# Four banks for maxima and projections, two for scores, and a reordered attention and feed-forward start

## The reference

```
x = x + attn_a(layernorm(x))   # causal, 32 query heads of 16, one key and value head, alibi bias
x = x + ffn(layernorm(x))      # router picks 1 of 32 hidden units in each of 56 blocks
x = x + attn_b(layernorm(x))   # 32 query and 8 key heads of 128, rope, window of 128
x = x + ffn(layernorm(x))

scores = q @ k.T * 16**-0.5 + slope * (pos_k - pos_q), causal;  attn_a = softmax(scores) @ v @ Wo
inter  = z @ c1.T @ c2.T;  idx = argmax of each block of 32;  ffn = relu(z @ w1[idx]) @ w2[idx]
```

## Time and profile before

| | us |
|---|---|
| median of 3 runs | 3085.81 |
| profiled execution | 3086.43 |
| its span, first to last instruction | 3084.6 |
| causal attention, 0 to | 591.7 |
| first feed-forward's router result of batch 0, batch 1 | 624.8, 771.3 |
| second feed-forward's, batch 0, batch 1 | 2640.4, 2785.1 |
| mean granted TensorE clock | 0.936 of full |

### The profile page before, as it was taken

One profiled execution on the slowest core, in us unless ns is written; L12 is line 12 of the kernel. 1 busy time (PEld: TensorE's weight loads), 2 busy tenths in 40 slices (PEclk: granted clock), 3 DMA queues, 4 the chain that ended last, 5 costly groups with the idle time before them and its releaser, 6 DMA issues. The chain is left out here.

```text
span 3084.6 us, 41728 instructions
## 1 busy us (share of the span) xinstructions
PE 2678.1 (87%) x14452; PEld 2053.9 (67%) x14452; DVE 2074.2 (67%) x4129; ACT 1121.8 (36%) x2436; POOL 976.9 (32%) x716
## 2 busy tenths in 40 slices
PE   3879898567989979999999987999999998589899
PEld 2444454255767757888888865788888886467677
DVE  2745645255777577778778757777877875657766
ACT  1345345222122244444444434444444443221221
POOL 1112011134222234444444423444444441342222
PEclk7799899778999999999999999999999999789999
DMA  5133332400000011110101100111010101100000
GB/s 189 31 107 84 81 106 59 140 1 0 1 0 0 23 35 35 35 34 27 32 9 34 34 29 8 35 35 34 27 32 8 34 21 44 63 1 15 14 14 14
DMA packets 112462, 117.64 MB, mean 38 GB/s; under 512 B 7028, under 2 KB 83956, under 8 KB 112308
## 3 DMA queue, kind: packets, MB, share of 16 engines
q1 hardware_dynamic: 112340, 116.04, 12.4%
HBM read 93.21 MB, written 22.81 MB: 38 GB/s over the span
## 5 line engine op out<-in xcount | busy, mean ns | idle before, releaser
L1762 POOL TENSOR_TENSOR rope_straight<-rope_straight,rope_crossed 128x512 f32<-128x512 f32 x160 | 206.8, 1292 | 478.4 <-DVE rope_crossed L1571 478.4
L520 POOL TENSOR_TENSOR f_hidden_low<-f_hidden,f_hidden_high 128x512 fp32r<-128x512 f32 x112 | 144.3, 1288 | 603.0 <-ACT f_hidden_high L468 603.0
L1667 ACT ACTIVATE probs<-probs,exp_bias 128x256 f32<-128x256 f32 (+1 forms) x512 | 240.7, 471 | 167.9 <-DVE exp_bias L1553 167.5
L896 DVE TENSOR_REDUCE a_max<-a_work 128x1 f32<-128x384 f32 (+3 forms) x352 | 209.6, 637 | 115.6 <-PE a_work L787 108.2
L261 PE MATMUL f_hidden_sum<-f_z_high,f_w_high 128*128 128x512 f32 x448 | 195.4, 436 | 75.7 <-POOL f_w_low L539 64.3
L1001 ACT ACTIVATE a_probs<-a_scores 128x512 f32<-128x512 f32 x320 | 173.0, 599 | 172.8 <-PE a_scores L801 95.9
L1412 PE MATMUL proj<-y_high,wq_high 128*128 128x512 f32 x512 | 213.3, 417 | 18.4 <-DVE y_low L1541 12.0
L782 PE MATMUL a_work<-a_keys,a_queries 64*128 64x256 f32 (+3 forms) x512 | 148.9, 443 | 71.9 <-DMA a_queries<-a_q_stacked 40.4
L1412 PE MATMUL w_sum<-o_high,wo_high 128*128 128x512 f32 x512 | 203.8, 398 | 7.6 <-DVE xt L1595 4.7
L372 DVE SCALAR_TENSOR_TENSOR f_hidden<-f_hidden_sum,f_mask_turned 128x512 f32<-128x512 f32 x112 | 77.0, 687 | 189.3 <-ACT f_mask_turned L463 172.2
L1412 PE MATMUL proj<-y_low,wq_high 128*128 128x512 f32 x512 | 204.0, 398 | 0.0
(11 more groups left out here) (239 smaller groups left out, 7683.8 us busy)
## 6 DMA issues: line engine op xcount, KB each, us to landing
a_queries<-a_q_stacked SPq DMA_DIRECT2D x16, 1024.0 KB, 6.3
wq_raw<-in_L_attn_b_wq SPq DMA_DIRECT2D x32, 512.0 KB
wo_raw<-in_L_attn_b_wo SPq DMA_DIRECT2D x16, 1024.0 KB, 6.8
a_q_stacked<-a_q_part_high SPq DMA_DIRECT2D x32, 256.0 KB
f_w_raw<-in_L_ffn_w SPq DMA_DIRECT2D x14, 512.0 KB, 10.1
f_w_raw<-in_L_ffn_w2t SPq DMA_DIRECT2D x14, 512.0 KB, 10.9
xt<-n_L_attn_a_hidden_states SPq DMA_DIRECT2D x4, 1024.0 KB, 29.3
a_q_stacked<-a_q_part_low SPq DMA_DIRECT2D x16, 256.0 KB
```

What stands on the lines that cost most here:

```text
L520: e.tensor_tensor(hl[:, j % 2], hm[:, :], f32(hh[:, j % 2]), ALU.subtract).then_inc(hl_ready, 1)
L896: e.tensor_reduce(mx[:, t % 2, to:to + nh], bank, AX.X, ALU.max).then_inc(work_free[k], 1)
L1667: e.activation(part, part, ACT.Exp, bias=bias[:, n % 2, t:t + 1], scale=SM_SCALE, accum_out=total[:, n % 2, t:t + 1]).then_inc(exp_done, 1)
L1762: e.tensor_tensor(ra[:, slot], ra[:, slot], rb[:, slot], ALU.add).then_inc(roped, 1)
```

## The change

In both feed-forward stages: `first_router` takes the place of `router_first(None)`; z of the first batch is normalised in four pieces; the squares stand ahead of the router constants on ACT; the constants' low parts are made by POOL instead of DVE; the w1 splits run two chunks ahead, the w2 splits one as before.

In the causal attention: `WORK` 4 and `SCORE` 2; new `SEARCH`, `OPENS` and `CLOSES`, and a `SEARCH_FIRST` for batch 0; tile 1's maxima of batch 0 move into the loop; the layer norm of batch 1 stands ahead of the loop, that of batch b+2 in slots 12 to 17; SP's list is reordered and x is loaded in pieces; the last batch's first three query tiles (`EARLY` = 384 columns) are divided and projected (`WoA`) apart from the last one, whose sums go from SBUF to SBUF, with half of its stores issued by ACT.

```diff
@@ ffn, TensorE
+            def first_router():
+                bank, full = aux_write(e, None, "T")
+                e.wait_ge(c_low, 1)
+                for d in range(DT):
+                    e.wait_ge(zh_ready, d + 1)
+                    e.matmul(bank[0:CROWS, :], c1h[:, d, :], zh[:, d, :], start=d == 0, stop=False)
+                    e.matmul(bank[0:CROWS, :], c1l[:, d, :], zh[:, d, :], start=False, stop=False)
+                    e.wait_ge(zl_ready, d + 1)
+                    mm = e.matmul(bank[0:CROWS, :], c1h[:, d, :], zl[:, d, :], start=False, stop=d == DT - 1)
+                mm.then_inc(full, 1)
@@ ffn, ScalarE (high_w1) and GpSimd (low_w1), in a chunk
                     if first and c + 1 < NCH:
-                        high_w1(c + 1)
+                        if c + 2 < NCH:
+                            high_w1(c + 2)
                         high_w2(c + 1)
@@ ffn, ScalarE before the loop
-            e.wait_ge(c_in, 32)
-            e.copy(c1h[:, :, :], c1_raw[:, :, :]).then_inc(c_high, 1)
             for d in range(DT):
                 e.wait_ge(first_centred, d + 1)
                 e.activation(first_squares[d], zf[:, d], ACT.Square).then_inc(first_squared, 1)
+            e.wait_ge(c_in, 32)
+            e.copy(c1h[:, :, :], c1_raw[:, :, :]).then_inc(c_high, 1)
             e.copy(c2s[:, :], c2_raw[:, :]).then_inc(c_high, 1)
             seed(None)
             high_w1(0)
             high_z(None)
             high_t(None)
+            high_w1(1)
             high_w2(0)
@@ ffn, GpSimd before the loop
+            e.wait_ge(c_high, 1)
+            e.tensor_tensor(c1l[:, :, :], c1_raw[:, :, :], f32(c1h[:, :, :]), ALU.subtract).then_inc(c_low, 1)
+            e.wait_ge(c_high, 2)
...
+            e.tensor_tensor(c2s[rest, :], c2_raw[rest, :], f32(c2s[rest, :]), ALU.subtract).then_inc(c_low, 1)
             low_w1(0)
+            low_w1(1)
             low_w2(0)
@@ causal_attention
-WORK, SCORE = 3, 3
+WORK, SCORE = 4, 2
+EARLY = S - P
-        SEARCH = {0: (2, 4), 1: (2, 4), 2: (2, 4), 3: (2, 4), 4: (3, 3), 5: (3, 3), 6: (3, 3), 7: (3, 3), 8: (3, 2),
-                  9: (3, 2), 14: (4, 2), 15: (4, 2), 16: (5, 3), 17: (5, 3), 18: (5, 2)}
-        OPENS = {4: ("mT", 2), 9: ("Vt", 0), 10: ("mT", 3), 16: ("mT", 4), 19: ("mT", 5)}
-        CLOSES = {0: ("mean", 0), 3: ("var", 0), 7: ("KV", 0), 8: ("Q", 0), 9: ("Q", 1), 10: ("Q", 2), 11: ("Q", 3),
-                  12: ("Wo", 0), 13: ("Wo", 1), 14: ("Wo", 2), 15: ("Wo", 3)}
+        SEARCH = {0: (2, 2), 1: (2, 2), 2: (2, 2), 3: (3, 3), 4: (3, 2), 5: (3, 2), 6: (3, 3), 7: (3, 2), 8: (3, 2),
+                  9: (3, 2), 10: (4, 2), 11: (4, 2), 12: (5, 2), 13: (5, 2), 14: (5, 2), 15: (5, 2), 16: (6, 2),
+                  17: (6, 3), 18: (6, 2), 19: (6, 3)}
+        SEARCH_FIRST = SEARCH | {0: (1, 4), 1: (1, 4)} | {s: (2, 4) for s in range(2, 6)} | {s: (3, 4) for s in range(6, 10)}
+        OPENS = {3: ("mT", 2), 4: ("Vt", 0), 10: ("mT", 3), 13: ("mT", 4), 17: ("mT", 5)}
+        CLOSES = {0: ("KV", 0), 2: ("Q", 0), 3: ("Q", 1), 5: ("Q", 2), 7: ("Q", 3), 9: ("Wo", 0), 11: ("Wo", 1),
+                  12: ("mean", 0), 13: ("Wo", 2), 14: ("Wo", 3), 15: ("var", 0)}
@@ plan
+            yield "small", "mean", 1, 0
+            yield "small", "var", 1, 0
-            for t in range(2):
-                for i in range(MAX_PAIRS[t]):
-                    yield "max", 0, t, i
-                yield "small", "mT", 0, t
+            for i in range(MAX_PAIRS[0]):
+                yield "max", 0, 0, i
+            yield "small", "mT", 0, 0
...
+                    if b == 0 and s in (1, 5):
+                        yield "small", "mT", 0, 1 if s == 1 else 2
...
             yield "pv", NB - 1, QUADS - 1
+            for d in range(DT):
+                yield "small", "WoA", NB - 1, d
@@ causal_attention, VectorE: last batch and tail
+                    if b == NB - 1 and p == 28:
+                        e.wait_ge(o_stored[0], 16 * OUT_DMAS * 2 * NB)
+                        e.wait_ge(o_stored[1], 16 * OUT_DMAS * (2 * NB - 1))
+                        e.reciprocal(sums[0:96, :], sums[0:96, :]).then_inc(inv_ready, 1)
+            e.wait_ge(o_stored[1], 16 * OUT_DMAS * 2 * NB)
+            e.reciprocal(sums[96:, :], sums[96:, :]).then_inc(inv_ready, 1)
@@ causal_attention, ScalarE: tail
+            store_out(e, NB - 1, 3, 1)
+            for m in range(DT):
+                high_out(NB - 1, m, slice(0, EARLY))
@@ causal_attention, SyncE: the loop and the end
-            send_max(0, 1)
+            e.dma_start(wo_raw[:, :, :], wo.rearrange("(t p) n -> p t n", p=P)).then_inc(wo_in, 16)
+            load_x(2)
...
+                if more:
+                    send_keys(b + 1)
+                if b == 0:
+                    send_max(0, 1)
...
+            e.wait_ge(inv_ready, NB)
+            for m in range(DT):
+                e.wait_ge(at_low, (NB - 2) * DT + m + 1)
+            load_last([0, 1, 2])
+            store_out(e, NB - 1, 3, 0)
+            e.wait_ge(inv_ready, NB + 1)
+            load_last([3])
```

More of the change, by code:

```diff
@@ L622, in causal_attention @@
         x_in = [sem(f"x_landed{b}") for b in range(NB)]
+        x_first, ones_landed, eye_landed = [sem(f"x_first_landed{d}") for d in range(DT)], sem("ones_landed"), sem("eye_landed")
         x_summed, sq_ready, sq_added, centred = sem("x_summed"), sem("sq_ready"), sem("sq_added"), sem("centred")
@@ L648, in of_batch, with searches @@
                 return (kind, b + i // ST, i % ST) if b + i // ST < NB else None
-            return (kind, b + 1, i) if b + 1 < NB else None
-        def searches(b, s, part):
-            if s not in SEARCH:
-                return
-            t, n = SEARCH[s]
-            if b + t // ST >= NB:
-                return
-            done = sum(k for r, (u, k) in SEARCH.items() if u == t and r < s)
-            for i in range(n * part // 4, n * (part + 1) // 4):
-                yield "max", b + t // ST, t % ST, done + i
-        def plan():
+            ahead = 2 if kind in ("mean", "var") else 1
+            return (kind, b + ahead, i) if b + ahead < NB else None
+        def plan():
+            done = {}
+            def searches(b, s, part):
+                t, n = (SEARCH if b else SEARCH_FIRST).get(s, (0, 0))
+                tile = b + t // ST, t % ST
+                if tile[0] < NB:
+                    for _ in range(n * part // 4, n * (part + 1) // 4):
+                        done[tile] = done.get(tile, 0) + 1
+                        yield "max", *tile, done[tile] - 1
             yield "small", "mean", 0, 0
@@ L713, in heads_in, with store_out @@
             return 4 if t == 0 else 2 if t == 1 else 1
+        def store_out(e, b, qt, half):
+            par, q = qt % 2, slice(qt * P, (qt + 1) * P)
+            e.wait_ge(o_copied, b * 2 * ST + qt * 2 + half + 1)
+            for j in range(4):
+                row, first = col_tile(half, j), (HEADS * half + 4 * j)
+                to = o_dram[b, first * AD:(first + 4) * AD, q].rearrange("(h d) q -> d h q", d=AD)
+                e.dma_start(to, ot[row:row + AD, par, half]).then_inc(o_stored[par], 16)
+            if b == NB - 1:
+                e.wait_ge(inv_stored, 16 * (NB - 1))
+                to = sums[AH * qt + HEADS * half:AH * qt + HEADS * (half + 1), :]
+            else:
+                to = sums_dram[b, HEADS * half:HEADS * (half + 1), q]
+            if half:
+                for c in range(2):
+                    e.dma_start(to[8 - 8 * c:16 - 8 * c], ot[64 * c + AD:64 * (c + 1):32, par, half])\
+                        .then_inc(o_stored[par], 16)
+            else:
+                e.dma_start(to, ot[AD::32, par, half]).then_inc(o_stored[par], 16)
         block = st.enter_context(nc.Block())
@@ L833, in _ @@
                     weigh(*step)
-            tail = [*(x[:, :] for x in work), sbank[0][:, :]]
+            tail = [x[:, 0:P] for x in work]
             for k, bank in enumerate(work):
@@ L924, in _ @@
                         low_weights(2, wkvl[:, :, 32:KV], w_raw[:, :, NQ:NQ + AD], wkvh[:, :, 32:KV])
+                    if step in (["var", 0, 0], ["var", 1, 0]):
+                        inverse_std(step[1], chain)
+                        for d in range(DT):
+                            normalise(step[1], d)
                     if step == ["var", 0, 0]:
-                        inverse_std(0, chain)
-                        for d in range(DT):
-                            normalise(0, d)
+                        for d in range(1, DT, 2):
+                            e.wait_ge(zh_ready, d + 1)
+                            e.tensor_tensor(zl[:, d], zf[:, d], f32(zh[:, d]), ALU.subtract).then_inc(zl_ready, 1)
                 elif kind == "max":
@@ L1241, in _ @@
                     load_queries(b + 1, 1)
-                store_out(b, 2)
+                send_max(b, 3)
+                if b == 0:
+                    load_x(3)
                 if more:
                     load_queries(b + 1, 2)
```

(3 more changed lines are left out.)

263 lines of the change are left out of this document (139 added, 124 removed).

## The result

The kernel after takes 2989.73 us (median of 4 runs, 2985.85 to 2992.66), the kernel before 3086.65 beside it: ratio 0.9686, 95% interval 0.9669 to 0.9703. The forecast was 2953, so the direction and the large terms held, and of 133 us of gain 97 came. The measured time lies 3 us inside the upper edge of the stated range (2925 to 2993).

| stage | before | after | gain | forecast |
|---|---|---|---|---|
| causal attention, from 0 | 591.7 | 567.0 | 24.7 | 42.5 |
| first feed-forward, start | 33.1 | 28.8 | 4.3 | 6 |
| its first batch | 146.5 | 109.4 | 37.1 | 41.2 |
| window attention | 1547.9 | 1554.1 | -6.2 | 0 |
| second feed-forward, start (from its first centring) | 25.3 | 21.9 | 3.4 | 4.3 |

What follows compares the result with a forecast made beforehand. No engine is full over the whole span, so each stage was read alone. Gains of 41.2 + 39.2 + 6 + 4.3 + 11 + 8 + 14 + 5 + 4.5 = 133.2 us took 3086.4 to 2953; range 2925 to 2993.

Steps and rivals of the forecast that it cites:

- rival 2: Causal attention: two score banks and late turning of maxima eat the even search, attention gains nothing; 2992 us; chance 10%.
- w1 ahead: Both feed-forward stages: PE no longer waits for w1 splits, first batches come down towards the second; gain 41.2 + 39.2 us.
- I charge 3 us per stage: Feed-forward first batches: 3 us deducted per stage for sums of squares queued on POOL behind splits and the colder start.
- rival 1: Feed-forward first batches: DVE, its operations falling behind POOL's splits, becomes the bound; 32 us lost, 2985 us; chance 10%.
- Start of the feed-forward: Both feed-forward starts: router matmuls follow z quarter by quarter; gain 6 us in the first stage, 4.3 in the second.
- Kernel start and batch 0: Causal attention: earlier queries and first maxima, less late turning of maxima, end batch 0 at 211 instead of 222; gain 11 us.
- Batches 1 to 3: Causal attention: fewer waits for maxima, less two score banks' cost; gains of 8, 14 and 5 us, bounds together -10 and 45.
- even search: Attention batches: two or three pairs of maxima in all slots, instead of four in slots 0 to 3 and none in 10 to 13.
- only 1 to 2 us: Attention batches: with Q's last projection two slots ahead of use, 1 to 2 of 5.7 us of PE's query wait go.
- Tail: End of causal attention: three quarters of the columns come early, 30.2 us behind the last weighing instead of 34.8; gain 4.5 us.
- 1.5 for the last matmuls: Attention tail: 1.5 us for PE's last matmuls, one term of the 30.2 us behind the last weighing.
- PE would wait for exps at every pair: Rival 3, attention: PE waits for the pair before's exps at each of 160 pairs; 3161 us at worst; chance 2%.

Runs made afterwards that it cites:

- Experiment 9: Kernel after with each POOL low part of w1 and w2 made by two instructions of 512 columns instead of one of 1024: 2978.06 us, ratio 0.9647.
- experiment 6: Kernel after with ACT's copies of the last batch's outputs two pairs of scores later, from pair 14 instead of 12: 2979.42 us, ratio 0.9626.
- experiment 3: Kernel after with three banks for maxima and projections and three for scores, as before: 2990.46 us, ratio 0.9685.
- (4): Kernel before with four banks for maxima and projections and two for scores, nothing else: 3056.24 us, ratio 0.9905.
- 8: Kernel before with four and two banks and all of the feed-forward's edits, none of the attention's other edits: 2985.15 us, ratio 0.964.
- (7): Kernel after with the maxima spread over the slots as before, the first ten slots of batch 0 kept: 2989.74 us, ratio 0.9662.
- Experiment 5: Kernel after with DVE's last reciprocal ahead of its four additions of early results, own semaphores for the last quarter's loads: 2977.68 us, ratio 0.9633.
- experiments 2: Kernel before with w1 split one chunk further ahead in both feed-forward stages and nothing else: 3011.10 us, ratio 0.9759.
- experiments 1: Kernel before with all of the feed-forward's edits and none of the attention's: 3013.77 us, ratio 0.9756.
- experiment 11: Kernel after with the start of the feed-forward as before, w1 staying one chunk ahead: 2986.09 us, ratio 0.9671.

## Why the prediction was right in kind, and its gain 36 us too high

The four figures to explain are 17.8 us of gain that the attention lacks, 9.5 that the two first batches lack, 2.6 that the starts lack, and 6.2 that the window attention lost. That rival 2's number, 2992, is nearer to the measured one than 2953 is chance: its terms (w1 in full, the attention at nothing) did not come.

**w1 ahead: mechanism right, the charge for the lock too small.** "I charge 3 us per stage" was read from the later chunks, where one operation falls behind one split. It was 7.1 (44.2 - 37.1) and 8.4: in the first two chunks POOL's list (two splits, then, in chunk 0, three sums) runs without a gap and catches two operations of one chain, and there PE has no lead. Experiment 9 shows it: halves give back 4.9 and 6.0. It is rival 1, at a third of its price: `L385` averaged 1.37 us in the first stage's first batch (0.85 with halves), over its mark of 1.3, `L358`'s successor 1.03.

**Start of the feed-forward:** 4.3 and 3.4 against 6 and 4.3, as said.

**Kernel start and batch 0:** 16.2 against 11. First scores at 82.4 (forecast near 80), and the batch took 123.4 us (forecast 131); the waits for landing maxima were 3.8, 3.9 and 1.5 us, less than the 6 each that were charged.

**Batches 1 to 3: the failed part.** 0.5, 13.4 and -2.5 against 8, 14 and 5. The forecast listed what moved in DVE's, PE's and SP's lists but not ACT's copies of the outputs, from pair 16 to 12, ahead of the loads they need: SP issues `load_out` behind stores and sends, and POOL's first product was ready 3.6 us late. That is 10.5 us of PE's waits (2.64, 3.89, 3.93); in experiment 6 the longest is 1.0, and batches 1 and 2 are 11.0 us shorter together. Second, it took bank split and even search for two gains. They are two cures of one wait: the max steps stand 27.1 us for `a_max` before, 12.6 with the new search and three banks (experiment 3), 6.9 with the banks alone (4) and 4.5 with both. In time, with the old search the banks bring 29 to 36 us (experiments 4 and 8), with the new one nothing (3), and the search with four banks nothing (7). Third, the wait for queries went from slot 14 to slot 10 with the maxima that need them, at 12.0 and 11.2 us for the slot, as the text had said that "only 1 to 2 us" would go.

**Tail:** -2.9 against 4.5. The step that failed is "1.5 for the last matmuls": the terms before it came out (9.3 us to the early matmuls, 10.3 for them, 5.0 instead of 7.3 from the reciprocal to the last ones), but these took 10.5, and 5.5 even at full clock. The order of DVE's program was seen rightly (the reciprocal did stand behind four additions, at 550.03), but not what it does to PE: 6.6 us idle, and then 48 matmuls at half clock (1.2 GHz). Experiment 5.

**Not forecast:** 6.2 us in the window attention, whose code is the same. Its cause is open (below).

**Readings that were off, without weight in the sum:** PE is busy 82.5% in batch 0, not 87 to 91 (99.5 of 120.6 us); and `L365` ended 0.55 us behind `L539`, not 0.4. Its argument that "one wait covers one split" did not hold in the chunk shown above, where two waits covered two splits.

The rival that the attention gains nothing fell as a whole (24.7 us came), though for batches 1 and 3 and the tail taken together it was right. That PE would wait for exps at every pair fell too: 24.6 us in 31 pieces over 160 pairs.

## What to carry to other kernels

Two edits that cure the same wait don't add: try each alone before both are costed, and let more buffers stand first, as it is the simpler. Of a reordered list, follow every engine's copy of it to the instruction that waits for a transfer: an instruction put too early on an in-order engine (a copy on ACT, four additions on DVE) stops all that stands behind it, and where PE stood long it pays again at the lower clock (the tail). Where POOL and DVE share a stretch, try POOL's long operations in two: here two stages gained 4.9 and 6.0 us by it.

## What the runs showed of the hardware

A matmul of 128 columns was 0.11 us behind the one before at full clock (experiment 5) and 0.21 at half, and those of 256 columns in the window attention of the kernel after were 0.12 apart: halving the columns from 256 saved next to nothing, so the 48 late matmuls of the tail are dearer than their columns tell.

The window attention took 1547.9, 1547.8 and 1548.0 us in before and experiments 2 and 4, and 1550 to 1561 in all others. Some of its pieces can be seen. One is four DVE operations, of which POOL's split catches the last or not. It is caught in experiments 1 and 8 alone, twice in each. Before, and in experiment 1:

```profile
1172.05 1.08 DVE L1560 TENSOR_SCALAR probs<-probs,exp_sum_inverse 128x128 f32<-128x128 f32 x4
1172.82 2.56 POOL L1769 TENSOR_TENSOR wkv_low<-wkv_raw,wkv_high 128x1024 fp32r<-128x1024 f32 x1 [3.05 <-ACT wkv_high L1690]
```

```profile
1130.88 3.27 DVE L1588 TENSOR_SCALAR probs<-probs,exp_sum_inverse 128x128 f32<-128x128 f32 x4
1131.65 2.35 POOL L1797 TENSOR_TENSOR wkv_low<-wkv_raw,wkv_high 128x1024 fp32r<-128x1024 f32 x1 [3.05 <-ACT wkv_high L1718]
```

The last of the four started 0.04 us ahead of POOL in the first and 0.06 behind it in the second, and took 0.35 or 2.44 us. In the kernel after it is not caught. There, a matmul group at the border of two batches started 6.8 us late with nothing in the trace to wait for, against 3.8 before. It was 6.6 to 7.2 us late in every kernel that has both the new attention and the new start of the feed-forward, and 3.8 to 4.2 in every kernel that lacks either. The other piece is the clock: the same 8008 matmuls kept PE busy 6.7 us longer, at a clock of 0.98 instead of 0.99. Before and after:

```profile
1067.10:2615.10 1548.00, 1433.88 (x8008) 1204.06 (x8008) 1178.39 (x2882) 674.41 (x1690) 620.73 (x464) 0.99 0.09 28
1001.10:2555.20 1554.10, 1440.60 (x8008) 1209.46 (x8008) 1177.91 (x2881) 674.13 (x1690) 620.56 (x464) 0.98 0.09 29
```

Experiment 5 had the late group (7.2 us) with the clock and the PE time of before (1434.7), and its stage took 1550.8; experiment 11 had a group of 4.0 us at the lower clock, and 1554.4. Why the group is late, and why the clock is lower, stays open; no run isolated it.
